# A graph network kernel: two quads share a fifth gather, and two smaller moves of work between ScalarE and VectorE

## The reference

```python
# block 0 (GIN)
e   = edge_attr @ W_edge + b_edge
msg = relu(x[src] + e)
h   = x + segment_sum(msg, dst)
h   = relu(h @ W1 + b1) @ W2 + b2
x   = layernorm(x + relu(batchnorm(h)))
# block 1 (GCN), three layers, self loops included, norm = dinv[src] * dinv[dst]
for W, b in layers:
    h = relu(segment_sum((h @ W.T)[src] * norm, dst) + b)
x   = layernorm(x + h)
```

## Time and profile before

| | us |
|---|---|
| median of 3 runs | 3689.67 (3687.28 to 3690.27) |
| the profiled execution | 3683.0 |
| its span, first to last instruction | 3681.2 |
| PE, PE weight load, ACT, DVE, POOL busy | 3196.1, 3071.9, 2920.5, 2819.9, 2373.0 |

### The profile page before, as it was taken

The page is one execution under the profiler, slowest core; times in us unless marked ns, Lnnn a source line. Parts: engine busy times, 40 slices in busy tenths (PEclk is TensorE's granted clock), DMA queues, the critical chain, the costliest instruction groups (busy, mean ns, idle before and its releaser), DMA issues. The chain is left out here.

```text
span 3681.2 us, 88209 instructions
## 1 busy us (share of the span) xinstructions
PE 3196.1 (87%) x24644; PEld 3071.9 (83%) x24644; DVE 2819.9 (77%) x7975; ACT 2920.5 (79%) x6007; POOL 2373.0 (64%) x2467
## 2 busy tenths in 40 slices
PE   4999999999993444459999997999999979999997
PEld 3999999999983444449999997999999979999997
DVE  5999999999986787756666664666666568888886
ACT  1777777777775888858888886788888859999999
POOL 3655555555525666647777775777777677777772
PEclk8999999999996555579999999999999989999999
DMA  4666666666636999967777775777777679999996
GB/s 114 191 178 177 185 181 180 181 181 179 184 113 224 347 353 340 348 196 241 239 236 239 236 239 180 223 241 237 239 238 235 203 247 304 301 299 298 297 297 210
DMA packets 654360, 858.82 MB, mean 233 GB/s; under 512 B 136335, under 2 KB 515882, under 8 KB 654256
## 3 DMA queue, kind: packets, MB, share of 16 engines
q1 hardware_dynamic: 556954, 652.14, 53.7%
q0 software_dynamic: 94080, 205.08, 19.9%
q10 hardware_dynamic: 3222, 0.43, 0.1%
HBM read 639.00 MB, written 257.52 MB: 244 GB/s over the span
## 5 line engine op out<-in xcount | busy, mean ns | idle before, releaser
L492 POOL DMA_INDIRECT rows<-x_in,node_i x490 | 581.3, 1186 | 442.8 <-DVE raw L1046 291.5
L492 POOL DMA_INDIRECT rows<-gb_scratch,node_i x490 | 502.6, 1026 | 198.8 <-issue 133.8
L492 POOL DMA_INDIRECT rows<-x_scratch,node_i x490 | 499.1, 1019 | 188.2 <-issue 130.1
L492 POOL DMA_INDIRECT rows<-ga_scratch,node_i x490 | 499.4, 1019 | 176.7 <-issue 158.4
L504 DVE TENSOR_SCALAR gcn_select<-iota,place 128x256 fp32r<-128x256 f32 (+2 forms) x980 | 365.5, 373 | 221.3 <-ACT gcn_rows_hi L1453 214.7
L520 PE MATMUL gcn_agg_ps<-gcn_select,gcn_rows_hi 128*128 128x256 f32 (+2 forms) x1960 | 502.7, 290 | 18.4 <-DVE gcn_rows_lo L1424 18.4
L534 PE MATMUL gcn_h_ps<-g_hi,gcn_agg_hi 128*128 128x256 f32 x1568 | 456.5, 291 | 62.7 <-ACT gcn_h_ps L1439 61.3
L520 PE MATMUL gcn_agg_ps<-gcn_select,gcn_rows_lo 128*128 128x256 f32 (+2 forms) x1960 | 484.4, 288 | 0.0
L1415 DVE TENSOR_TENSOR gcn_agg_lo<-gcn_agg_ps,gcn_agg_hi 128x1024 fp32r<-128x1024 f32 x196 | 240.0, 1224 | 267.9 <-ACT gcn_agg_hi L1447 267.9
L534 PE MATMUL gcn_h_ps<-g_lo,gcn_agg_hi 128*128 128x256 f32 x1568 | 444.8, 284 | 0.0
L534 PE MATMUL gcn_h_ps<-g_hi,gcn_agg_lo 128*128 128x256 f32 x1568 | 444.1, 283 | 0.0
(11 more groups left out here) (189 smaller groups left out, 11201.9 us busy)
## 6 DMA issues: line engine op xcount, KB each, us to landing
own<-x_t_in SPq DMA_DIRECT2D x196, 256.0 KB, 2.7
h_scratch<-h2t SPq DMA_DIRECT2D x196, 256.0 KB, 3.4
h2t_in<-h_scratch SPq DMA_DIRECT2D x98, 512.0 KB, 5.1
x_sb<-x_q_in SPq DMA_DIRECT2D x98, 512.0 KB, 6.7
x_scratch<-x SPq DMA_DIRECT2D x98, 512.0 KB, 5.6
gcn_own<-x_scratch SPq DMA_DIRECT2D x98, 512.0 KB
ga_scratch<-gcn_h SPq DMA_DIRECT2D x98, 512.0 KB, 3.3
gcn_own<-ga_scratch SPq DMA_DIRECT2D x98, 512.0 KB
```

Of the source, the lines that this page charges most:

```text
L492: pool.indirect_dma_start(out=c["rows"][0:n, slot, b], out_offset=None, in_=source[:, :], in_offset=bass.IndirectOffsetOnAxis(ap=c["node"] ...
```

## The change

Three edits are joined.

1. **The shared fifth gather** (three node passes). The fifth block of an odd quad is now read backwards: a reversed copy of the edge list (`edges_back`) and of the edge attributes (`attr_back`) is loaded, so that its tail lies from partition 127 down, while the even quad's lies from 0 up. The table adds the two `node` entries of the fifth block for the even quad, so one indirect DMA brings both tails, and in a node pass the odd quad issues four gathers. Before the even quad's fifth gather POOL waits for `rows_ready` of one quad more. ACT and DVE split only 4 blocks for an odd quad; PE reads the even quad's split block. The selection matrices and all matmuls stay. `gin_pass` still gathers five blocks for each quad (all of 128 rows now), and pays for the tables: two more window DMAs for each group of four quads, one more attribute DMA for one pair in four, and one more DVE operation in the table. `search` gets a longer chain, which tests that two tails together have at most 128 edges (over the drawn edges, at most 60).
2. **ACT's order in `gcn_pass`**: eviction (lag 5), bias (now lag 3), `agg_hi` (lag 3), `rows_hi` (lag 1).
3. **`last_pass`**: the fourth tile of `y` is written by DVE at the end of its step, with a semaphore `fourth_ready` that SP's store and DVE's reuse of `res` wait for.

```diff
@@ gather_quads
-        for b in range(BLOCKS):
-            n = LAST_ROWS if b == BLOCKS - 1 else P
-            pool.indirect_dma_start(out=c["rows"][0:n, slot, b], out_offset=None, in_=source[:, :],
-                                    in_offset=bass.IndirectOffsetOnAxis(ap=c["node"][0:n, quad, b:b + 1], axis=0),
+        shared = tables is None
+        for b in range(BLOCKS - (quad % 2 if shared else 0)):
+            if shared and b == BLOCKS - 1 and quad >= QUAD_RING:
+                pool.wait_ge(rows_free, (quad - QUAD_RING + 2) * per)
+            pool.indirect_dma_start(out=c["rows"][:, slot, row_block(slot, b) if shared else b], out_offset=None, in_=source[:, :],
+                                    in_offset=bass.IndirectOffsetOnAxis(ap=c["node"][:, quad, b:b + 1], axis=0),
                                     bounds_check=bound, oob_is_err=False).then_inc(gathered[slot], 16)
@@ load_windows
+                if k % 2:
+                    back = eng.value_load(c["backs"][0:1, bass.ds(q, 1)], min_val=0, max_val=NPAD)
+                    eng.dma_start(c["window"][:, bass.ds(q, 1), BLOCKS - 1].rearrange("p o t -> p (o t)"),
+                                  dram["edges_back"][bass.ds(back, P), :]).then_inc(landed, 16)
@@ gin_pass, table
+                    nc.vector.tensor_tensor(node[:, 0:GROUP_QUADS:2, BLOCKS - 1], node[:, 0:GROUP_QUADS:2, BLOCKS - 1],
+                                            node[:, 1:GROUP_QUADS:2, BLOCKS - 1], ALU.add).then_inc(table_steps, 1)
+                    dve.wait_ge(table_steps, number * TABLE_STEPS + 5)
@@ search, DVE
+                nc.vector.tensor_scalar(first_edge[:], start_row, 0.0, float(E), ALU.max, ALU.min).then_inc(chain, 1)
+                dve.wait_ge(chain, 14)
+                nc.vector.tensor_scalar(c["backs"][0:1, 0:NQ], first_edge[:], -1.0, float(NPAD), ALU.mult, ALU.add)
...
+                dve.wait_ge(chain, 19)
+                nc.vector.tensor_reduce(nbroken[:], broken[:], AX.X, ALU.add).then_inc(chain, 1)
@@ gcn_pass, DVE
                         for k in range(BLOCKS):
-                            select_columns(nc, c, quad, select[:, b], [k])
-                            last = nc.vector.tensor_tensor(rows_lo[:, b, k], c["rows"][:, s, k],
-                                                           rows_hi[:, b, k].bitcast(F32), ALU.subtract)
+                            last = select_columns(nc, c, quad, select[:, b], [k])
+                            if k < quad.new:
+                                last = nc.vector.tensor_tensor(rows_lo[:, quad.split_block(k)], c["rows"][:, s, row_block(s, k)],
+                                                               rows_hi[:, quad.split_block(k)].bitcast(F32), ALU.subtract)
@@ gcn_pass, ACT (the eviction at(5) moves ahead of this)
-                    if quad := at(4):
+                    if quad := at(3):
                         if quad.has(2):
                             act.wait_ge(h_ready, quad.before(2))
                         for j in range(4):
                             last = nc.scalar.activation(h_ps[:, quad.b, j], bias[:], ACT.Identity,
                                                         scale=c["root"][:, quad.tile(j)])
                         last.then_inc(biased, 1)
...
-                        act.wait_ge(gathered[s], quad.landed(BLOCKS))
+                        act.wait_ge(gathered[s], quad.landed(quad.new))
                         if quad.has(2):
                             act.wait_ge(agg_done, quad.before(2))
-                        nc.scalar.copy(rows_hi[:, b], c["rows"][:, s]).then_inc(rows_rounded, 1)
+                        nc.scalar.copy(rows_hi[:, quad.held], c["rows"][:, s, 0:quad.new]).then_inc(rows_rounded, 1)
@@ last_pass, DVE, at the end of the step
+                    if quad := at(7):
+                        b, s = quad.b, quad.slot
+                        dve.wait_ge(shift_ready, quad.done(2))
+                        if quad.has(2):
+                            dve.wait_ge(stored[b], quad.twos * 16)
+                        nc.vector.tensor_scalar(y[:, b, 3], res[:, s, 3], rs[:, b, 3:4], shift[:, b, 3:4],
+                                                ALU.mult, ALU.add).then_inc(fourth_ready, 1)
@@ last_pass, ACT
-                        for j in range(4):
+                        for j in range(3):
                             last = nc.scalar.activation(y[:, b, j], res[:, s, j], ACT.Identity,
                                                         bias=shift[:, b, j:j + 1], scale=rs[:, b, j:j + 1])
```

More of the change, by code:

```diff
@@ L302, in search @@
         rel = m.sb("rel", [P, LIMITS - 1])
-        broken = m.sb("broken", [P, 8])
+        broken = m.sb("broken", [P, 9])
+        first_edge = m.sb("first_edge", [1, NQ])
+        edges_of = m.sb("edges_of_quad", [1, NQ])
+        tail_of = m.sb("tail_of_quad", [1, NQ])
+        tails = m.sb("tails_of_two", [1, NQ // 2])
+        too_many = m.sb("too_many", [1, NQ // 2])
         nbroken = m.sb("nbroken", [P, 1])
@@ L408, in __init__ @@
         self.twos = group * (QUAD_RING // 2) + place // 2
+        self.new = BLOCKS - place % 2
+        first = (0, 6, 1, 6)[place]
+        self.held = slice(first, first + self.new)
     def done(self, per=1):
@@ L519, in sum_columns @@
             for rows in (rows_hi, rows_lo):
-                last = nc.tensor.matmul(out[:, h, first:end], rows[:, b, k, h * P:(h + 1) * P],
+                last = nc.tensor.matmul(out[:, h, first:end], rows[:, quad.split_block(k), h * P:(h + 1) * P],
                                         select[:, b, k, 0:end - first], start=False,
@@ L1434, in step @@
                 def step(at):
-                    if quad := at(4):
+                    if quad := at(5):
+                        s = quad.slot
+                        act.wait_ge(dense_done, quad.done())
+                        if quad.has(QUAD_RING):
+                            act.wait_ge(stored[s], quad.turn * 16)
+                        for j in range(4):
+                            last = nc.scalar.activation(h[:, s, j], h_ps[:, quad.b, j], ACT.Relu,
+                                                        scale=c["dinv2"][:, quad.tile(j)])
+                        last.then_inc(h_ready, 1)
+                    if quad := at(3):
                         if quad.has(2):
@@ L1572, in step @@
                             dve.wait_ge(y_ready, quad.before(QUAD_RING))
+                            dve.wait_ge(fourth_ready, quad.before(QUAD_RING))
                         if quad.has(2):
@@ L1602, in step @@
                         dve.wait_ge(rows_rounded, quad.done())
-                        for k in range(BLOCKS):
-                            last = nc.vector.tensor_tensor(rows_lo[:, b, k], c["rows"][:, s, k],
-                                                           rows_hi[:, b, k].bitcast(F32), ALU.subtract)
+                        for k in range(quad.new):
+                            last = nc.vector.tensor_tensor(rows_lo[:, quad.split_block(k)], c["rows"][:, s, row_block(s, k)],
+                                                           rows_hi[:, quad.split_block(k)].bitcast(F32), ALU.subtract)
                         last.then_inc(rows_ready, 1)
+                    if quad := at(7):
[5 more added lines that the diff above has]
+                                                ALU.mult, ALU.add).then_inc(fourth_ready, 1)
                 quad_pipeline(dve, step)
```

76 lines of the change are left out of this document (48 added, 28 removed).

## The result

The changed kernel takes 3571.3 us (median, 3566.7 to 3573.5) against 3689.5: a ratio of 0.9679, interval 0.9662 to 0.9696. The profiled execution took 3571.7, its span is 3570.0.

The account below looks back on a forecast made before the run. POOL, its gap counted in, was taken to bound the gcn passes and ACT the last pass. Gcn -68, last pass -29 and added work +3 gave -94 us, from 3689.7 to 3596; range 3578 to 3650.

Parts of the forecast that it names:

- ends of the passes: Shorter starts and ends of passes: no term in the forecast sum, 3 us in the low end of the range.
- What bounds before: POOL with its gap bounds both gcn passes at 6.60 us a quad, ACT the last pass at 7.05.
- Gcn, 68 us: Both gcn passes: the shared gather takes 6.60 us a quad to 6.25, PE's 6.21 plus 0.5%; bounds 39 and 76.
- ACT's order at 0: Gcn: the new order has the bias ready before PE reads it, costed at 0; without that cover 0.27 us a quad.
- The added wait at 0: Node passes: POOL's longer wait before an even quad's fifth gather costs 0, since POOL keeps up.
- rival 3: Node passes: the wait for the shared gather closes a loop, gcn at 7.03 us a quad, 3776 us; chance 0.04.
- The fourth tile and the splits, 29 us: Last pass: DVE's tile and four-block splits take 7.05 us a quad to 6.75; bounds 35 and 5.
- DMA engines at 6.51 to 6.70: Last pass: time a quad the DMA engines need once the shared gather takes 0 to 0.19 us away.
- rival 2: Last pass: the DMA engines fill, pace stays at 7.00 us a quad, saving 5, total 3620 us; chance 0.10.
- Rivals 1 and 4: Gcn: PE misses its pace, 6.45 us a quad, 3635 us (0.13); or gathers lengthen to 1.186 us, 3681 (0.04).
- What it adds, 3 us: Search 1.7 us and start of gin_pass 1 us, the other 24 groups 0; bounds 2 and 10.
- lost cover: Gin_pass: table work of the other 24 groups, 0.25 us each, no longer hidden beside a full PE: 6 us.

Follow-up runs that it names:

- e1: Changed kernel with ACT's old order in gcn and all four tiles of y on ACT, leaving the shared gather and tables: 3606.6 us, ratio 0.9781.
- e8: Kernel before with 8 of PE's 24 product matmuls a quad left out in the node passes: 3684.6 us beside 3690.0.
- e2: Kernel before with ACT's new order in gcn and the fourth tile of y on DVE: 3640.7 us, ratio 0.9872.
- e6: Changed kernel with 8 of PE's 24 product matmuls a quad left out in the node passes: 3518.6 us.
- e4: Changed kernel without POOL's added wait ahead of an even quad's fifth gather: 3566.8 us, ratio 0.9675.
- e5: Changed kernel with POOL's added wait made two quads longer: 3708.3 us, ratio 1.0046.
- e10: e6 with less work for ACT (squares) and DVE (low part of gathered rows) in the last pass, same transfers: 3468.3 us.
- e3: Kernel before with only the changed search, tables and gin_pass, five gathers a quad and both old orders: 3699.9 us, ratio 1.0039.
- e9: e4 with SP's window DMAs for the third group issued after the first four pairs' loads: 3567.5 us, ratio 0.9673.

## Why the prediction was right or wrong, point by point

The engines that bound before and after were named rightly. Sizes were wrong: the forecast gave 94 us and 118.2 were measured, a gain larger by 24. Three terms failed: the pace was taken with margins that no wait justified, the ends of the passes had no term, and the price was put too low.

| term | forecast | measured |
|---|---|---|
| pace in the steady part, gcn and last | 68 + 29 | some 74 + 38 |
| ends of the passes | 0 (3 in the low end of the range) | some 10 + 5 |
| what the change adds | -3 | -8.6 |

- **What bounds before**: right. POOL with its gap in gcn (e1 takes gathers away and gcn falls, e8 lightens PE and it doesn't), ACT in the last pass (e2).
- **Gcn, 68 us**: the mechanism was right (e6, e8), the size off. It brought 84.2. The pace came out at 6.22, 0.01 above the 6.21 read from one quad; the 0.5% on top was for hand-overs that didn't occur, 6 us. With 0.38 us a quad the pace gives 0.38 x 194 = 73.7; the other 10.5 lie at the ends of the passes, for which the sum had no term. Part of that is ACT's order: e1 puts it at 8.3 for both passes. What the rest is stays open.
- **ACT's order at 0**: right for the pace. But its price without POOL's cover, 0.27 us a quad, was wrong: it was a wait that PE had time for, since POOL held it back anyway. With rows in time, the old order keeps PE full too (e1). And 0 left out the 8.3 at the ends.
- **The added wait at 0 and rival 3**: right; e4 shows the 0, and e5 where the loop closes.
- **The fourth tile and the splits, 29 us**: it brought 42.6. PE's floor was 6.66, not 6.69: that sum took the product and transposes from a quad that began after idle, 4.19 us, and in the changed kernel they take 4.16. The 6.75 put 0.06 on top for resources near full, and they cost nothing: 9 us together. Some 5 us are again at the ends. ACT at 6.55 (491.92/75.1) and DVE at 6.34 (476.34/75.1) stand where 6.44 and 6.44 were taken; the tile on DVE takes 0.32 us between starts (3108.47 to 3108.79 in e6), where 0.35 was taken. That the two come to 6.65 as a loop was not seen: the text had 6.62 for DVE's even quad and compared it with PE only.
- **DMA engines at 6.51 to 6.70, rival 2**: wrong as a limit; e10 passes the same transfers at 6.14. The share is no linear measure of what is left. It read 0.95 at 299 GB/s and 1.02 at 344 GB/s in e10. The Trainium skill's figure of about 358 GB/s ("DMA: Bandwidth & Descriptors", Where 436 GB/s comes from) agrees in so far as no fortieth of a span, on the page of any run, read over 353, and by it the forecast would have been 6 us lower.
- **Rivals 1 and 4**: neither. PE reached its pace, and gathers took 1018 ns in all node passes, with DVE at 95%.
- **What it adds, 3 us**: some 8 to 9, near the upper bound of 10 (e3's medians say 14, and 9 to 20 by their interval). Two parts failed. The prologue was put at 2.7 and is 5.1 at the first gather: the search is 2.75 later rather than 1.7, and the first table 2.2 more. Named were the two window DMAs ahead of it; missed was that SP also issues the third group's windows before the first pair's loads, which e9 shows to cost. And the other 24 groups were put at 0 beside a full PE; the runs show 3.0 us there, about half of the 6 that the prediction gave for a lost cover.
- **Profile against median**: the 94 us were read from a profiled execution 6.7 us under the median and taken off the median. That was sound: the passes that the change speeds up were of usual length in that trace, and its norm pass was the shortest of 14 (478.7 against 482.3 to 484.6 in the three others without the new tables).
- **The range** missed by 7 us, and the ends of the passes alone are more than that: its low end took 76 and 35 for the pace, which measured 74 and 38, and 2 for the price, which measured 8.6, but 3 for the ends, which measured some 15. Its high end was rounded to 3650 where the sum gives 3656.

## What to carry to other kernels

Where the next limit is an engine whose work is seen without idle in the trace, its pace can be taken as it is read; a margin for "everything is near full" needs a wait that shows it. Shortening a step can also shorten the start and end of a pass, here by some 15 us over three passes, so give the ends a term of their own in the sum and in the range. Two engines that hand work to each other can have a limit of their own when their steps differ from quad to quad: add the longer step of each along the loop and compare that with the means. A DMA added to a queue delays what is issued behind it there, here the first load of rows by 7.1 us, so list that queue's order up to the first load that the bottleneck needs. And work added beside an engine that is 99.9% busy isn't free for that reason: here it cost 3 us of 900.

## What was not expected of the hardware

The DMA busy share passed 1 (1.02 at 344 GB/s, e10) while no engine was seen to wait for a transfer in that stretch, and the same mix read 0.95 at 299 GB/s before. A share near 1 in this profile didn't mean that the engines were the bound: at 0.98 a quad of the last pass took 6.66 us (317 GB/s), and in e10 6.14.
